# Expert matrices W1, W3 and W2 with an arrival signal and a time of release each, in a mixture-of-experts kernel on one Trainium2 core

## The reference, cut to what matters

```python
scores = softmax(xf @ Wg.T)                      # xf: 4096 tokens x 256
expert_weights, expert_indices = top_k(scores, 2)
expert_weights = expert_weights / expert_weights.sum(-1, keepdims=True)
# for each token t and each expert e that it chose:
h1 = W1[e] @ x + b1[e] + B1[e] @ (A1[e] @ x)     # 256 -> 512
h3 = W3[e] @ x + b3[e] + B3[e] @ (A3[e] @ x)     # 256 -> 512
g  = silu(h1) * h3
y  = W2[e] @ g + b2[e] + B2[e] @ (A2[e] @ g)     # 512 -> 256
out[t] += expert_weight * y
```

## Time and profile before

| | |
|---|---|
| three timed runs | 1158.61, 1159.03, 1160.38 us; median 1159.03 |
| the profiled execution | 1158.17 us, of which the span of the trace is 1156.5 |
| PE busy | 1066.6 us, 92% of the span |
| PE weight load busy | 921.1 us, 80% |
| DVE busy | 786.2 us, 68% |
| POOL busy | 427.5 us, 37% |
| ACT busy | 392.3 us, 34% |
| `moe`, first to last PE work | about 639 to 1003 us from the span's start |

### The profile page before, as it was taken

How to read it: one execution, slowest core, us unless ns; L and a number is a source line. 1 busy time by engine, 2 the same in 40 slices (tenths; PEclk the granted TensorE clock), 3 DMA queues, 4 the chain that set the end, 5 groups by cost and what they waited for, 6 DMA issues and landing times. The chain is left out here.

```text
span 1156.5 us, 20362 instructions
## 1 busy us (share of the span) xinstructions
PE 1066.6 (92%) x6338; PEld 921.1 (80%) x6338; DVE 786.2 (68%) x1743; ACT 392.3 (34%) x768; POOL 427.5 (37%) x408
## 2 busy tenths in 40 slices
PE   5999999999999993599994899999999989899996
PEld 4899999999998993477773688888888878777875
DVE  5688887887878673556764477777777757663755
ACT  3645554463646331242210222222222212342210
POOL 2846454463645430074474000000000000088875
PEclk8999999999999995699997899999999989899998
DMA  9354563675466238463573715152454241275554
GB/s 266 98 191 161 171 207 127 192 181 199 125 181 194 102 139 202 131 187 96 181 222 111 259 51 183 55 188 70 173 187 172 72 169 47 85 151 86 85 114 91
DMA packets 115475, 170.70 MB, mean 148 GB/s; under 512 B 17200, under 2 KB 89520, under 8 KB 115248
## 3 DMA queue, kind: packets, MB, share of 16 engines
q1 hardware_dynamic: 95408, 122.19, 34.5%
q0 software_dynamic: 19968, 47.23, 14.2%
HBM read 98.24 MB, written 71.14 MB: 146 GB/s over the span
## 5 line engine op out<-in xcount | busy, mean ns | idle before, releaser
L1714 PE MATMUL wide<-expert_ring,xsT 128*128 x852 | 232.5, 409 | 7.0 <-POOLq L1696 5.5
L1714 PEld LDWEIGHTS wide<-expert_ring,xsT 128*128 128x128 f32 x852 | 153.2, 192 | 35.3 <-issue 8.0
L1773 ACT ACTIVATE gsT<-bank 128x512 fp32r<-128x512 f32 x71 | 42.6, 600 | 255.7 <-PE bank L1733 255.7
L1601 POOL DMA_DIRECT2D expert_ring<-experts_scratch x24 | 17.0, 714 | 285.1 <-issue 285.1
L1714 PEld LDWEIGHTS bank<-expert_ring,gsT 128*128 128x128 f32 x852 | 111.8, 188 | 6.6 <-issue 0.3
L1714 PE MATMUL bank<-expert_ring,gsT 128*128 x852 | 113.8, 282 | 0.1
L1826 DVE TENSOR_TENSOR h<-wide,expert_bias 128x512 f32<-128x512 f32 x71 | 49.1, 692 | 81.5 <-PE wide L1714 80.6
L1256 POOL DMA_INDIRECT slot_rows_scratch<-ring,slot x64 | 67.7, 1057 | 69.1 <-DVE slot L1561 48.4
L1242 POOL DMA_INDIRECT first_half<-slot_results_scratch,slot x32 | 52.1, 1628 | 89.1 <-DMA first_half<-x_scratch 80.3
L444 POOL TENSOR_TENSOR folded_matrix<-fold,folded_matrix 128x512 fp32r<-128x512 f32 x48 | 63.9, 1339 | 39.8 <-ACT folded_matrix L636 37.0
L460 PE MATMUL wide<-xnT,w 128*128 128x512 f32 x234 | 60.5, 400 | 0.0
(11 more groups left out here) (279 smaller groups left out, 2407.0 us busy)
## 6 DMA issues: line engine op xcount, KB each, us to landing
experts_scratch<-folded_matrix SPq DMA_DIRECT2D x24, 1024.0 KB, 5.2
expert_ring<-experts_scratch POOLq DMA_DIRECT2D x24, 1024.0 KB, 7.4
raw<-in_expert_weights SPq DMA_DIRECT2D x24, 512.0 KB, 7.2
xs_ring<-slot_rows_scratch SPq DMA_DIRECT2D x71, 128.5 KB, 2.1
slot_results_scratch<-ys_ring SPq DMA_DIRECT2D x71, 128.0 KB, 2.1
slot_rows_scratch<-zeros SPq DMA_DIRECT2D x23, 385.5 KB, 7.1
ring<-xn_scratch SPq DMA_DIRECT2D x32, 257.0 KB, 3.3
xn_scratch<-xb SPq DMA_DIRECT2D x16, 512.0 KB, 7.3
```

Of the source, the lines that this page charges most:

```text
L1714: ins = mm(o, parts[i], moving, start=(first and q == 0), stop=(last and q == 2))
L1773: return nc.scalar.activation(o, i, ACT.Copy)
```

## The change

Each of the three matrices gets its own `expert_in` and its own `expert_ready` semaphore. The bias transfer is cut in two: b1 and b3 (512 KB) follow W1 and count with it, b2 (128 KB) follows W2 and counts with it. `PARTS_IN` says how much a complete part adds. For rank e of 2 and more, POOL now waits for `h_taken` of the last tile of rank e - 2 before W1, biases and W3, signals these two, then waits for `y_taken` and starts W2 and b2. PE waits for a signal before each of the two hidden products and before `out_rows`. In the first attention, `LE:3` is gone and the two bias transfers stand at `LE:0` and `LE:2`. `xs_ring` has 6 places (`ROUND`) instead of 8. Three semaphores that nothing waited for are gone.

```diff
-            keep["expert_in"] = [held.enter_context(nc.semaphore(f"expert_in{i}")) for i in range(2)]
+            keep["expert_in"] = [[held.enter_context(nc.semaphore(f"expert_in{i}_{m}")) for m in range(3)] for i in range(2)]
...
-        SC:26 SC:27 YS:9 LE:3 SC:28 YS:10 YS:11 YS:12 YS:13 SC:29 YS:14 SC:30 YS:15 SC:31
+        SC:26 SC:27 YS:9 SC:28 YS:10 YS:11 YS:12 YS:13 SC:29 YS:14 SC:30 YS:15 SC:31
...
-    arrived = keep["expert_in"][j % 2]
-    if m < 3:
-        at = slice(2 * HID * m, 2 * HID * (m + 1))
-        pool.dma_start(keep["experts"][:, 1 - j % 2, :, at].bitcast(F32),
-                       scr["experts"][bass.ds(e, 1), :, :, at].rearrange("e p h n -> (e p) h n")).then_inc(arrived, 16)
-    else:
-        pool.dma_start(keep["expert_bias"][:, j % 2, :],
-                       io["expert_bias"][bass.ds(e, 1), :].to_broadcast([P, BIASES])).then_inc(arrived, 16)
...
+    arrived, slot = keep["expert_in"][j % 2][m], j % 2
+    at = slice(2 * HID * m, 2 * HID * (m + 1))
+    pool.dma_start(keep["experts"][:, 1 - slot, :, at].bitcast(F32),
+                   scr["experts"][bass.ds(e, 1), :, :, at].rearrange("e p h n -> (e p) h n")).then_inc(arrived, 16)
+    if m != 1:
+        at = slice(0, 2 * HID) if m == 0 else slice(2 * HID, BIASES)
+        pool.dma_start(keep["expert_bias"][:, slot, at],
+                       io["expert_bias"][bass.ds(e, 1), at].to_broadcast([P, at.stop - at.start])).then_inc(arrived, 16)
+
+
+PARTS_IN = (32, 16, 32)
...
-    ROUND = 8
+    ROUND = 6
...
+            def arrived(e, m):
+
+                pool.wait_ge(keep["expert_in"][e % 2][m], PARTS_IN[m] * (e // 2 + 1))
+                pool.sem_inc(expert_ready[m], 1)
+
             for e in range(E):
-                if e == 1:
-                    load_expert(pool, io, keep, scr, e)
+                if e:
+                    of = expert_of_rank(pool, keep, e)
                 if e >= 2:
 
                     end = pool.value_load(keep["rank_end"][0:1, e - 2:e - 1], min_val=0, max_val=SLOTS_T)
+                    hold(pool, loader_held, h_taken, end + 2)
+                for m in (0, 1):
+                    if e:
+                        load_expert_part(pool, io, keep, scr, e, m, of)
+                if e < 2:
+                    if e:
+                        load_expert_part(pool, io, keep, scr, e, 2, of)
+                    for m in range(3):
+                        arrived(e, m)
+                else:
+                    for m in (0, 1):
+                        arrived(e, m)
+
                     hold(pool, loader_held, y_taken, end + 2)
-                    load_expert(pool, io, keep, scr, e)
-                pool.wait_ge(keep["expert_in"][e % 2], 64 * (e // 2 + 1))
-                pool.sem_inc(expert_ready, 1)
+                    load_expert_part(pool, io, keep, scr, e, 2, of)
+                    arrived(e, 2)
...
-                    pe.wait_ge(expert_ready, e + 1)
+                pe.wait_ge(expert_ready[m], e + 1)
...
                 pe.wait_ge(y_taken, j + 1)
+                pe.wait_ge(expert_ready[2], e + 1)
...
-                dve.wait_ge(expert_ready, e + 1)
+                dve.wait_ge(expert_ready[0], e + 1)
```

More of the change, by code:

```diff
@@ L982, in route @@
         w_in, c_in, row_in = sem("l1_weights_in"), sem("l1_cols_in"), sem("l1_rows_in")
-        spread_ready, rowprod, folded = sem("ln1_bias_spread"), sem("l1_bias_products"), sem("l1_folded")
+        spread_ready, rowprod = sem("ln1_bias_spread"), sem("l1_bias_products")
         high, split = sem("l1_weights_high"), sem("l1_weights_split")
@@ L1050, in _ @@
             dve.wait_ge(row_in, 48)
-            tt(bv[:], bv[:], S[0][:, 0:H1], ALU.add).then_inc(folded, 1)
-            tt(cols[:, 4:8], cols[:, 4:8], S[1][:, 0:EC], ALU.add).then_inc(folded, 1)
-            tt(cols[:, 8:10], cols[:, 8:10], S[1][:, 512:514], ALU.add).then_inc(folded, 1)
+            tt(bv[:], bv[:], S[0][:, 0:H1], ALU.add)
+            tt(cols[:, 4:8], cols[:, 4:8], S[1][:, 0:EC], ALU.add)
+            tt(cols[:, 8:10], cols[:, 8:10], S[1][:, 512:514], ALU.add)
             for p in range(2):
@@ L1154, in attention @@
         else:
-            chosen, counted, within_ready, slots_ready, ranks_ready = (
-                sem("experts_chosen"), sem("choices_counted"), sem("within_ready"), sem("slots_ready"), sem("ranks_ready"))
+            chosen, slots_ready, ranks_ready = sem("experts_chosen"), sem("slots_ready"), sem("ranks_ready")
             ring_in = [sem(f"ring_in{i}") for i in range(RINGS)]
@@ L1642, in moe @@
         assert nc.sbuf_base <= limit, (nc.sbuf_base, limit)
-        expert_ready, loader_held = sem("expert_ready"), keep["held"]["gpsimd"]
+        expert_ready, loader_held = [sem(f"expert_ready{m}") for m in range(3)], keep["held"]["gpsimd"]
         x_high, g_high = sem("slots_high_ready"), sem("gated_high_ready")
```

## The result

| | before | after |
|---|---|---|
| median of the timed runs | 1159.35 us (4 runs, 1158.61 to 1160.38) | 1148.15 us (4 runs, 1147.61 to 1149.83) |
| profiled execution, span of its trace | 1158.17, 1156.5 | 1148.09, 1146.4 |
| PE busy | 92% | 93% |

The ratio is 0.9905, with a 95% interval of 0.9888 to 0.9922. That is a gain of about 11.0 us, 9.0 to 13.0 by the interval. (A ratio here is worked out from the executions and is not quite the quotient of the two medians, which is 0.9903.) Two of the 28 executions of the kernel before that stand beside the first four experiments were slow ones of 1386 and 2761 us: they are in its median of 1169.22, which is 1169.14 without them, and in no ratio. The sign and the mechanism were forecast.

The account below looks back on a forecast made before the run. PE, 92% busy, was taken as the bound, losing removable time only in one stall on an expert's arrival. 1159.03 less the stall's 8.27, all other terms 0, gave 1150.8 us, range 1149.2 to 1153.2.

Parts of the forecast that it names:

- What bounds the kernel, and what the change removes: Expert block: PE, busy 92%, waits 5.5 us once at a W1 product for POOL's signal; the change removes that wait.
- What it costs today: Stalled round at rank 7: 13.16 us against a regular 4.89, loss 8.27, of it 5.46 idle and 2.8 slow clock.
- How the numbers follow: Whole kernel: scatter about 1149.5 to 1152.3 us, range 1149.2 to 1153.2 for eight of ten; faster by over 0.2%: 0.93.
- The bounds: Whole kernel: stated range of 1149.2 to 1153.2 us around the forecast median of 1150.8.
- Release, W2, signals: Expert loads: W1 starts 11.0 us earlier, W2 lands before its need; signals nearly suffice alone; whole 8.27 us goes, gains not added.
- More waits: PE, before W3 and `out_rows`: 142 added waits cost 0, at most 0.03 us each or 4.3 us.
- `xs_ring` with 6 places: Row loads: lead falls from 20.6 to 10.8 us against a longest landing of 7.7; spare 3.1 us, cost 0.
- The `LE` units: First attention: moved bias issues hold POOL 0.61 us each, hidden, one barely; sum 0, bounds -0.6 to +0.6 us.
- All of it between 929 and 975.: Sign of being right: the span 8.3 us shorter, all within the stretch from 929 to 975 us holding the stall.

Follow-up runs that it names:

- the first four experiments: Changed kernel unedited, with release and signals undone, with signals alone, with release alone; ratios to the kernel before 0.9894, 0.9989, 0.9931, 0.9915.
- w4_waits: Changed kernel with four more already satisfied waits in each PE round; 1148.33 us against 1148.12 for the changed kernel.
- e3_neither: Changed kernel with early release and separate signals undone, the rest of the change kept; 1168.02 us against 1169.22 for the kernel before.
- e3_again: Changed kernel with early release and separate signals undone, run once more on another chip; 1157.71 us against 1157.33 for the kernel before.
- b1_phase: The kernel before the change, unedited, run again for its trace; ratio 0.9998 to the kernel before.
- b2_phase: The kernel before the change, unedited, run once more for its trace; ratio 0.9995 to the kernel before.
- a3_phase: The changed kernel, unedited, run again for its trace; 1158.19 us, ratio 0.9895 to the kernel before.

## Why the prediction was wrong

*What bounds the kernel, and what the change removes.* Right. The only wait in the expert block that the change can reach is gone in all traces with either half of the change, and back in all traces with neither.

*What it costs today.* This is the term that was mis-sized, 8.27 us. It was worked out rightly for the one trace there was, and was taken as the fixed size of the stall. In three traces of the kernel before, the stalled round lost 13.16 - 4.90, 15.46 - 4.90 and 13.63 - 4.90, that is 8.3, 10.6 and 8.7 us, mean 9.2. The trace at hand had the smallest. (These are three executions on two chips, and the 10.6 alone lifts the mean above 9.) The changed kernel does not vary there: stretch C is 342.30 to 342.36 in five traces. Of the stall, clock and idle together had to be counted, as the prediction did. With the idle time alone it would have missed by half.

*How the numbers follow.* The range allowed 1149.5 to 1152.3 for the scatter, from the spread of three runs. (The sum itself is a little off: 1158.61 and 1160.38 less 8.27, with 0.6 us to each side, give 1149.7 to 1152.7.) The step that failed here is that everything outside the stall was put at nothing. The time behind a block border depends on how long the clock stays low there. That moved stretch D by up to 1.6 us in one and the same kernel, and by 1.02 us between the two executions. Mean stretch D is 149.91 in three traces of before and 149.37 in five of after.

The profiled pair accounts for 10.1 of the 11.2 us between the two first medians: 8.3 in the stalled round, 0.3 in the other rounds, 1.0 in stretch D by the clock, and 0.5 in stretches A and B. The other 1.1 us is how far the profiled executions lay from their medians (1.18 us below for before, 0.06 for after), and no trace shows where that is. So in the first measurement the part that is seen to go beyond the forecast is stretch D, and whether the untraced executions also had a longer stall is not known.

Over all traces, the stall of 9.2 us in the mean, 0.3 in the other rounds and 0.5 in stretch D make 10.0 us. The medians beside each other differ by 11.2, 9.5, 9.2, 10.0 and 9.8 us, 9.9 in the mean. That is what the traces account for. The five ratios of the changed kernel, 0.9905, 0.9894, 0.9914, 0.9898 and 0.9895, average 0.9901, which is a gain of 11.5 us. The interval of each holds 10.0 us, but where the 1.5 us between the two ways of reading belongs is open.

*The bounds.* With 10.6 us as the stall's upper bound, which only a later run showed, and the 1.3 us of scatter that the forecast allowed below its middle, the range would have begun at 1159.0 - 10.6 - 1.3 = 1147.1, and the time would have been inside.

*Release, W2, signals.* Right in direction, close in size. W1 started 10.3 us ahead of the last result (forecast 11.0). W2 started 1.1 us behind it (forecast 1.3), but that is luck: it was held by the landing of W3, a wait that the prediction left out. By the prediction's own bound for that landing (930.8) W2 could have started 3 us later than forecast, still ahead of its need. Both halves were shown to suffice alone, the release with 1 us to spare and the signals with none.

*More waits.* Taken as 0, and right. By w4_waits it is 0.0002 us each in the rounds, and at most 0.002 us with the block's end. The upper bound of 0.03 us was 15 times too high or more.

*`xs_ring` with 6 places.* Taken as 0, and in the trace of after no wait for rows stands behind the block's start. One place less costs 4 us, so the 3.1 us of spare that was worked out was real and not large.

*The `LE` units.* Not told apart by themselves. In e3_neither and e3_again they are in place, and the ratio to before is 0.9989 and 0.9995, with intervals of 0.9959 to 1.0019 and 0.9977 to 1.0013. By the narrower one they and the other parts together cost at most 1.5 us or bring at most 2.7.

*"All of it between 929 and 975."* Wrong: about 1.8 of the 10.1 us of the profiled pair lay elsewhere.

Open: what decides between the short and the long slow stretch. All five traces with the stall had the long one, of the nine without it four had the short and five the long. Three traces of the changed kernel had the one and two the other, so the change does not fix it. Whether the stall favours the long one is not shown. Open too is why the biases of rank 7 land 11 or 13 us after their issue.

## What to carry to other kernels

A stall on a transfer is worth its idle time plus the slow work behind it, and both vary from run to run: with one trace, give the stall a range that reaches well above what that trace shows, since the fix also removes the bad cases. An early release and a finer arrival signal often cure the same wait, so look at which of them alone brings the need behind the arrival, and do not add their gains. What they can add is room: here none or 1 us with either, over 10 us with both. A queue that waits for its own transfers to land before it starts the next one is a release too, so put that wait into the chain. When a ring is shortened, compare the new lead with the longest landing beside the heaviest transfers: here 10.8 us was enough for about 7, and 5.9 was not.

## What was not expected of the hardware

The granted clock, fallen behind the same idle stretch of 3.9 us at the same block border, stood at 0.50 for 3.25 us in one trace of the changed kernel (after) and for 6.75 us in another (a3_phase), with the same instructions. Over fourteen traces the slow stretch, with its edges, was 3.5 to 3.75 us or 7.0 to 7.25 us long, and never between. Four transfers with the same sizes, issued one behind the other from the same engine with an otherwise quiet queue, had their last landing 10.9, 13.1 and 11.0 us after its issue in three traces (before, b1_phase, b2_phase). In 68 rounds, 272 more waits that were already satisfied cost PE 0.05 us in all.
